# Exponentials of two score blocks per image moved to GpSimd and VectorE, and two kinds of turns moved off TensorE, in a ViT layer with a mixture of experts

## The reference

```
h = patches @ W.T + b + pos_embed                       # 16 images x 1024 tokens x 64
x = layernorm(h)
q, k, v = x @ Wq + bq, x @ Wk + bk, x @ Wv + bv         # 8 heads of 8
scores = q . k / sqrt(8) + col_bias[head, key]          # col_bias from 16384 edges
h = h + softmax(scores) @ v @ Wo + bo
t = layernorm(h)
probs = softmax(t @ router_w.T)                         # 8 experts, the best two are kept
out = h + t + sum_e combine[:, e] * (gelu(t @ w1[e] + b1[e]) @ w2[e] + b2[e])
```

## Time and profile before

| what | value |
|---|---|
| median of 3 runs | 1130.87 us (1130.76 to 1132.0) |
| the profiled execution's own time | 1132.75 us |
| its span, first to last instruction | 1130.7 us |
| TensorE busy (matmuls) | 1086.5 us, 96% |
| ScalarE busy | 1026.2 us, 91% |
| VectorE busy | 623.4 us, 55% |
| GpSimd busy | 130.8 us, 12% |
| mean granted TensorE clock | 0.995 |
| attention stage | about 48 to 991 us |
| expert stage | about 991 to 1130.7 us |

### The profile page before, as it was taken

One profiled execution on the slowest core, in us unless ns is written; L12 is line 12 of the kernel. 1 busy time (PEld: TensorE's weight loads), 2 busy tenths in 40 slices (PEclk: granted clock), 3 DMA queues, 4 the chain that ended last, 5 costly groups with the idle time before them and its releaser, 6 DMA issues.

```text
span 1130.7 us, 21748 instructions
## 1 busy us (share of the span) xinstructions
PE 1086.5 (96%) x7803; PEld 318.6 (28%) x7804; DVE 623.4 (55%) x1765; ACT 1026.2 (91%) x1127; POOL 130.8 (12%) x137
## 2 busy tenths in 40 slices
PE   3499999999999999999999999999999999999998
PEld 3122222222222222222222222222222222233333
DVE  8423465646464737374646465554646542476865
ACT  1299999999999999999999999999999999976654
POOL 3304011111111110102010101010101101000000
PEclk9899999999999999999999999999999999999999
DMA  2523131314141414241423232232323136049895
GB/s 55 128 59 67 55 85 46 88 41 109 30 119 31 107 43 105 46 105 46 104 46 95 56 94 56 74 76 66 84 58 76 42 85 152 16 136 241 236 246 164
DMA packets 73794, 100.78 MB, mean 89 GB/s; under 512 B 17276, under 2 KB 30076, under 8 KB 73660
## 3 DMA queue, kind: packets, MB, share of 16 engines
q1 hardware_dynamic: 71404, 98.73, 34.6%
q10 hardware_dynamic: 1776, 0.24, 0.1%
q0 software_dynamic: 480, 0.06, 0.1%
HBM read 57.67 MB, written 40.37 MB: 87 GB/s over the span
## 4 chain that ended last, share of the span: by engine, by line
PE 77%; ACT 10%; issue 6%; DVE 3%; DMA 2%; SPq 0%; ACTq 0%; POOL 0%; DVEq 0%; POOLq 0%
PE psum L1653 37%; PE psum L1637 21%; ACT probs L1369 10%; PE psum L1706 4%; PE psum L1730 4%; PE psum L743 2%; DMA m_cT<-cT_d 2%; PE psum L731 1%; PE psum L747 1%; PE psum L767 1%; PE psum L772 1%; PE psum L737 1%; PE psum L753 1%; PE psum L1716 1%; DMA x_d<-x2T 0%
## 5 line engine op out<-in xcount | busy, mean ns | idle before, releaser
L1369 ACT ACTIVATE probs<-psum 128x1024 f32<-128x1024 f32 x1024 | 941.1, 1241 | 26.5 <-PE psum L1637 26.4
L1653 PE MATMUL psum<-probs,VA 128*32 128x512 f32 x4096 | 547.0, 606 | 1.9 <-ACT probs L1369 0.4
L1637 PE MATMUL psum<-QA,KA 54*128 54x512 bf16 x2048 | 331.6, 385 | 8.4 <-issue 3.6
L1637 PEld LDWEIGHTS psum<-QA,KA 54*128 54x128 bf16 x2048 | 82.0, 93 | 484.9 <-ACT probs L1369 447.1
L1441 DVE STREAM_TRANSPOSE oT<-psum 128x512 f32<-128x512 f32 x64 | 45.9, 717 | 202.3 <-PE psum L1653 201.8
L1653 PEld LDWEIGHTS psum<-probs,VA 128*32 128x32 f32 x4096 | 81.8, 108 | 151.9 <-issue 130.9
L1404 ACT ACTIVATE probs<-psum,b 128x1024 f32<-128x1024 f32 x64 | 68.1, 1111 | 41.0 <-PE psum L1706 40.9
L1706 PE MATMUL psum<-m_x,w 64*128 64x512 f32 x256 | 61.6, 596 | 2.9 <-DMA m_cT<-cT_d 2.7
L1548 DVE TENSOR_TENSOR probs<-probs,psum 128x1024 f32<-128x1024 f32 x32 | 39.1, 1220 | 33.8 <-PE psum L1716 31.1
L1730 PE MATMUL psum<-probs,w 128*64 128x512 f32 x240 | 57.3, 598 | 0.0
L1308 POOL TENSOR_TENSOR p_rstd<-p_ve,neg_half 128x8 f32<-128x8 f32 x16 | 32.9, 2055 | 207.2 <-DVE p_ve L468 207.2
(11 more groups left out here) (180 smaller groups left out, 813.6 us busy)
## 6 DMA issues: line engine op xcount, KB each, us to landing
H_all<-comb_d SPq DMA_DIRECT2D x64, 256.0 KB, 5.5
QA<-q_parts_d SPq DMA_DIRECT2D x64, 192.0 KB
KA<-k_parts_d SPq DMA_DIRECT2D x64, 192.0 KB
q_parts_d<-qk_parts SPq DMA_DIRECT2D x32, 192.0 KB, 2.5
k_parts_d<-qk_parts SPq DMA_DIRECT2D x32, 192.0 KB, 2.7
xT<-in_xT SPq DMA_DIRECT2D x16, 256.0 KB, 2.7
q_parts_d<-qk_parts SPq DMA_DIRECT2D x32, 128.0 KB, 2.6
k_parts_d<-qk_parts SPq DMA_DIRECT2D x32, 128.0 KB, 2.5
```

The costliest lines, as they stand in the source:

```text
L1369: nc.scalar.activation(probs[:, k % PROB_BUFS, :], score_buf(buf_of(k)), ACT.Exp).then_inc(exped, 1)
L1637: last = pe.matmul(score_buf(buf_of(k))[:, (g % 2) * BANK:(g % 2 + 1) * BANK], KA[rows_of(h, SCORE_ROWS), h // 2, jt * P:(jt + 1) * P], QA ...
L1653: last = pe.matmul(o_acc[32 * g:32 * g + 32, :], VA[:, jt, h, :], probs[:, k % PROB_BUFS, (g % 2) * BANK:(g % 2 + 1) * BANK], start=(jt == ...
```

## The change

Quads 15 and 31 of each image (the last of each half of the heads) give their second block to a side path: `SIDE_QUADS = (15, 31)`, so ScalarE has 62 blocks per image. Its scores are computed by four auxiliary steps of one matmul each (`side_0` to `side_3`), long before the quad's own slot. VectorE drains each to SBUF times log2(e); GpSimd and VectorE then compute 2 to that power on 128x1024 float32: the rounded integer part, the fraction, a polynomial of degree five by ten GpSimd instructions per block in all (six with one tensor input, four with two), and the product with the power of two. The value matmuls of quads 15 and 31 read the result and wait for it (`side_done`).

`norm_t` and `post_t` go: VectorE makes the normalised rows in another order and turns them in 32x32 blocks (`turn_normal`, `turn_x2`), SyncE stores the result to DRAM with four DMAs and loads it as the transposed tile (`store_normal`, `load_normal`, `store_x2`, `load_x2`). `xnT` gets two buffers. The router's matmuls have the weights as the stationary side and write 32 rows each, and VectorE turns the logits. The rows of `comb_d` are stored by one DMA, in another order, in which the loads of L1242 read runs of 128 numbers rather than 512. Slots are moved, and `buf_of` is now a plain remainder counted over all images.

```diff
-BLOCKS = 2 * QUADS
+SIDE_QUADS = (15, 31)
+EXPS = [(q, half) for q in range(QUADS) for half in range(2) if not (half and q in SIDE_QUADS)]
+EXP_OF = {place: k for k, place in enumerate(EXPS)}
+BLOCKS = len(EXPS)
-AUX_SLOTS = {0: ("qk0", 0), 2: ("qk0", 1), 4: ("out_proj", 0), 6: ("out_proj", 1), 8: ("qk1", 0), 10: ("qk1", 1),
-             12: ("post_t", 0), 14: ("router", 0), 16: ("router", 1), 18: ("sq", 0), 19: ("embed", 0), 22: ("embed", 1),
-             24: ("v", 0), 26: ("v", 1), 28: ("combine_t", 0), 30: ("norm_t", 0)}
+AUX_SLOTS = {0: ("side_0", 0), 1: ("side_1", 0), 2: ("qk0", 0), 4: ("qk0", 1), 5: ("out_proj", 0), 7: ("out_proj",
+             1), 10: ("qk1", 0), 11: ("qk1", 1), 13: ("sq", 0), 16: ("side_2", 0), 18: ("side_3", 0),
+             19: ("router", 0), 21: ("embed", 0), 23: ("embed", 1), 25: ("v", 0), 26: ("v", 1), 30:
+             ("combine_t", 0)}
+FRACTION_SLOTS, POWER_SLOTS = (3, 19), (14, 30)
-CENTRE_SLOT, SCALE_SLOT, SPLIT_SLOT, SHIFT_SLOT, LEAD_SLOT, NORM_SLOT = 6, 10, 13, 20, 23, 28
-ROUTER_EXP_BLOCK = 36
-BUF_TURN = 38
+CENTRE_SLOT, SCALE_SLOT, SPLIT_SLOT, SHIFT_SLOT, LEAD_SLOT, NORM_SLOT = 8, 11, 16, 22, 24, 28
+ROUTER_EXP_BLOCK = 38
-COMBINE_SLOT, WEIGH_SLOT = 19, 22
+COMBINE_SLOT, WEIGH_SLOT = 21, 28
-G_SLOT = 26
+G_SLOT = 14
...
+            def side_round(b, side):
+                n = SIDES * b + side
+                g.wait_ge(aux_drained, aux_count(b, SIDE[2 * side + 1]))
...
+                g.tensor_scalar(side_n[:, :], side_y[:, n % 2, :], ROUNDER, None, ALU.add).then_inc(side_rounded, 1)
+            def side_terms(b, side, first, last):
...
+                    if c == 4:
+                        g.wait_ge(side_split, n + 1)
+                        g.tensor_scalar(side_p[:, :], side_f[:, :], POWER_TERMS[5], POWER_TERMS[4], ALU.mult,
+                                        ALU.add).then_inc(side_chain, 1)
+                    else:
+                        g.tensor_scalar(side_p[:, :], side_p[:, :], POWER_TERMS[c], None, ALU.add).then_inc(side_chain, 1)
+                    g.wait_ge(side_chain, base + 2 * (4 - c) + 1)
+                    g.tensor_tensor(side_p[:, :], side_p[:, :], side_f[:, :], ALU.mult).then_inc(side_chain, 1)
+                    g.wait_ge(side_chain, base + 2 * (4 - c) + 2)
+            def side_power(b, side):
+                g.tensor_scalar(side_y[:, n % 2, :].bitcast(I32), side_n[:, :], 1.5 * 2.0 ** 23, 2.0 ** 23, ALU.subtract,
+                                ALU.mult).then_inc(side_ready, 1)
...
+            def side_step(step, b, filled):
+                v.tensor_scalar(side_y[:, n % 2, i % 2 * BANK:(i % 2 + 1) * BANK], aux, LOG2E, LOWEST_POWER, ALU.mult,
+                                ALU.max).then_inc(aux_drained, 1)
+            def side_fraction(b, side):
+                v.wait_ge(side_rounded, n + 1)
+                v.scalar_tensor_tensor(side_f[:, :], side_n[:, :], ROUNDER, side_y[:, n % 2, :], ALU.subtract,
+                                       ALU.subtract).then_inc(side_split, 1)
+            def side_product(b, side):
+                v.wait_ge(side_ready, n + 1)
+                v.scalar_tensor_tensor(side_n[:, :], side_p[:, :], POWER_TERMS[0], side_y[:, n % 2, :], ALU.add,
+                                       ALU.mult).then_inc(side_done, 1)
...
                 link(v.tensor_copy(qk_parts[:, 0, :], qk[:, :]))
-                if bp:
-                    link(v.tensor_tensor(qk_rest[:, :], qk[:, :], qk_parts[:, 0, :], ALU.subtract))
                 v.tensor_tensor(squares[:, :], qk_parts[:, 0, :], qk_parts[:, 0, :],
                                 ALU.mult).then_inc(squares_ready, 1)
+                link(v.tensor_tensor(qk_rest[:, :], qk[:, :], qk_parts[:, 0, :], ALU.subtract))
...
-                    sp.dma_start(comb_d[bq].rearrange("t (r c i) -> c r t i", c=NCH // 2, i=32)[c],
-                                 combB[32 * c:32 * c + 32, :, :]).then_inc(comb_stored, 16)
+                sp.dma_start(comb_d[bq].rearrange("t (p i) -> p t i", i=32), combB[:, :, :]).then_inc(comb_stored, 16)
...
-                        sp.dma_start(wgt_rows[i][D * e:D * e + D, :].rearrange("p (t n) -> p t n", t=2),
-                                     comb_d[b].rearrange("t (e n) -> e t n", e=NX)[2 * m + e].partition_broadcast(D)).then_inc(rows_spread[i], 16)
+                        sp.dma_start(wgt_rows[i][D * e:D * e + D, :].rearrange("p (g n) -> p g n", n=P),
+                                     comb_d[b].rearrange("t (a e n) -> e (t a) n", a=QUARTERS, e=NX)[2 * m + e].partition_broadcast(D)).then_inc(rows_spread[i], 16)
```

The new order on GpSimd, one image:

```diff
                 def body(b):
+                    side_round(b, 0)
+                    if b:
+                        g.wait_ge(pv_done, QUADS * b)
+                        alone(g)
+                        copy_v(1)
                     add_bo(b)
+                    side_terms(b, 0, 4, 3)
                     if b:
                         post_pow(b - 1)
+                    side_terms(b, 0, 2, 1)
+                    side_power(b, 0)
...
                         prep_rq(b + 1)
+                    side_round(b, 1)
+                    side_terms(b, 1, 4, 3)
                     if b + 2 < NB:
                         prep_rstd(b + 2)
+                    side_terms(b, 1, 2, 1)
+                    side_power(b, 1)
```

More of the change, by code:

```diff
@@ L67 @@
 COMB_COPIES = ((0, 24), (24, 48), (48, 64))
-POST_UNITS = {2: "out_proj", 12: "post_t", 16: "router", 32: "combine_t"}
+POST_UNITS = {2: "out_proj", 16: "router", 32: "combine_t"}
 STATS_UNITS = {4: range(NCH // 2), 5: range(NCH // 2, NCH)}
@@ L241, in score_buf, with exp_at, exps_through, values_before @@
             return psum[:, 2 * BANK * i:2 * BANK * (i + 1)]
[L243 to L249, removed]
+        def exp_at(b, q, half):
+            return BLOCKS * b + EXP_OF[q, half]
+        def exps_through(b, q):
+            return exp_at(b, q, 0 if q in SIDE_QUADS else 1) + 1
+        def values_before(n):
+            return QUADS * (n // BLOCKS) + EXPS[n % BLOCKS][0] + 1
         o_acc = psum[:, 6 * BANK:7 * BANK]
@@ L415, in load_shift @@
                                  shift_row[heads, :]).then_inc(aug_loaded[hg], 16)
-            return (load_x, all_parts, first_parts, store_x2, store_tokens, store_combine, store_weights, load_rows, load_zeros,
-                    load_shift)
+            return (load_x, all_parts, first_parts, store_x2, load_x2, store_tokens, store_normal, load_normal, store_combine,
+                    store_weights, load_rows, load_zeros, load_shift)
         def pool_steps(g):
@@ L740, in aux_step @@
                     rows = slice(D * int(step[-1]), D * int(step[-1]) + D)
+                    if step == "qk0" and n >= 2:
+                        pe.wait_ge(xn_loaded, 16 * (n - 1))
                     for i in halves:
                         cols = slice(i * BANK // 2, (i + 1) * BANK // 2)
-                        last = pe.matmul(aux[:, cols], w_qk[rows, :, :].rearrange("k a e -> k (a e)"), xnT[rows, cols],
+                        last = pe.matmul(aux[:, cols], w_qk[rows, :, :].rearrange("k a e -> k (a e)"), xnT[rows, n % 2, cols],
                                          start=True, stop=True)
@@ L746, in aux_step @@
                     for c in chunks:
-                        last = pe.matmul(aux[:, c * P:(c + 1) * P], xnT[:, c * P:(c + 1) * P],
+                        last = pe.matmul(aux[:, c * P:(c + 1) * P], xnT[:, n % 2, c * P:(c + 1) * P],
                                          w_v[:, :, :].rearrange("k t e -> k (t e)"), start=True, stop=True)
-                elif step == "post_t":
-                    pe.wait_ge(x2_made, n + 1)
-                    alone(pe)
-                    for c in range(NCH // 2):
-                        last = pe.transpose(aux[:, c * P:(c + 1) * P],
-                                            x2[:, c, :, :].rearrange("p t d -> p (t d)"), ident[:, :])
                 elif step == "sq":
@@ L1191, in _ @@
                 steps = sync_steps(sp)
-                load_x, all_parts, first_parts, store_x2, store_tokens, store_combine, store_weights = steps[:7]
-                load_rows, load_zeros, load_shift = steps[7:]
+                load_x, all_parts, first_parts, store_x2, load_x2, store_tokens, store_normal, load_normal = steps[:8]
+                store_combine, store_weights, load_rows, load_zeros, load_shift = steps[8:]
                 def body(b):
-                    order = aux_order(b)
+                    if b:
+                        store_x2(b - 1)
+                        load_x2(b - 1)
                     if b + 1 < NB:
@@ L1277, in _ @@
                         load_weights(u + 2 * WEIGHT_BUFS - 2)
-                    if POST_UNITS.get(u - 1) == "post_t":
-                        sp.wait_ge(aux_drained, END + POST.index("post_t") + 1)
+                    if u == SCALE_UNIT + 1:
                         store_x2(NB - 1)
+                        load_x2(NB - 1)
```

(2 more changed lines are left out.)

283 lines of the change are left out of this document (191 added, 92 removed).

## The result

The changed kernel takes **1392.94 us** (median of 4 runs, 1391.74 to 1400.45), the kernel before 1131.43 us beside it: a ratio of 1.232, with a 95% interval of 1.229 to 1.235. It is 23% slower; forecast were 1112 us, with a range up to 1180.

A forecast was written before the change was run, and what follows sets the result against it. It took ScalarE (58.3 us) and TensorE (57.6 us), coupled by three score buffers, to bound the 58.8 us image. 1132.75 - 25.6 + 5 + 1.6 = 1113.8, with the median 1.9 lower: 1112 us, range 1100 to 1180.

The forecast's parts named there:

- The shared path: GpSimd and VectorE meeting in SBUF: perhaps ten meetings of 0 to 2.4 us, taken as 0.3 us per image, 5 in all.
- the two-input price: GpSimd operation with two inputs: 2.39 us for 1024 elements, upper end for the one-input float operations taken at 1.1.
- The second rival: GpSimd and VectorE take turns, TensorE waits for VectorE: 0 to 9 us per image, 1177 to 1250 us; chance 0.33.
- 0.908 us in a chain: ScalarE in attention: 62 exponentials per image, one following the other, 56.4 us of work, 1.8 less.
- the sum of -1.2 us: TensorE per image: transposes and router halves removed, new router, single scores and evacuation wait added, leaving 56.4 us of work.
- about 7: VectorE per image: drains, three-operand steps and turns, less two copies, add about 7 us, making 39.5 of 57.2.
- The period: Time per image in attention: 56.4 us on both engines plus 0.8 gives 57.2, 1.6 less, 25.6 for 16 images.
- SyncE at cost 0: SyncE's DMA queue: the added stores and loads of normalised rows and x2 delay nothing that is due, cost 0.
- Experts, +1.6: Expert stage: TensorE loses 1.4 us of work, weight rows read in shorter runs cost +3, net +1.6 us.
- the third rival: Expert stage: weight rows arrive late, DMA at its limit, +12 to +35 us, 1125 to 1147; chance 0.10.

The follow-up runs named there:

- experiment 6: k1 with one side block per image and the low part's split in slot 18, chain on VectorE (k5) or GpSimd (k6): 1147.1 and 1217.1 us.
- experiment 3: The kernel before with ten GpSimd products per image that nobody reads, or twice as many fills instead: 1255.3 and 1131.7 us.
- Experiment 1: The changed kernel with GpSimd's additions written as product and addition, and the last step likewise: 1348.3 us.
- k1: The kernel without a side block from experiment 4, with the load of normalised rows moved ahead in SyncE's queue: 1148.1 us, ratio 1.012.
- experiment 2: The changed kernel without the side path, 64 exponentials back on ScalarE, router, turns and slots kept: 1160.5 us.
- experiment 4: The changed kernel with weights stored in eight DMAs; no side block, one on GpSimd (fast forms), or one on VectorE: 1234.2, 1312.4, 1261.6 us.
- k5: k1 with one side block per image, whole chain on VectorE, split of the low part in slot 18: 1147.1 us, ratio 1.013.
- k6: k1 with the same side block and split slot as k5, but the chain on GpSimd in fast forms: 1217.1 us, ratio 1.075.

## Why the prediction was wrong

**The step that failed is "The shared path".** It had the right mechanism, from the right rows, and counted ten meetings of up to 2.4 us an image; then it put them down as 0.3 us, because "most fall where nothing is due". The side path as a whole cost 75.0 - 59.8 = 15.2 us per image against the kernel without one: TensorE waits for 12.5 us where it waited for 1.9, and is busy for 62.5 where it was for 57.9. What the runs put in its place is three things.
- Meetings don't fall here and there. GpSimd's chain is back to back, and so is VectorE's between a drain and a due point, so step after step of VectorE meets the next of GpSimd: scale, cast and squares in a row add 2.2 + 1.7 + 0.7 us (experiment 6). The argument that VectorE is idle for 26 us of an image was of no use: experiment 3 lost 9 us per image with VectorE far from full. A short step is lengthened like a long one: `comb`, 0.23 us before, takes 2.08 ahead of the wait for `combine_t`.
- The size of one meeting was too small as well. The bound of 2.4 us held for the products only; operations of 2.8 to 3.6 us were priced at 1.1, from the range's lower end. The text had given the two-input price as its upper end, and that too was passed. Experiment 1 puts this at 45 us of the total: in the fast forms GpSimd is busy for 39.7 us per image, where 39 were forecast, in the changed kernel for 59.
- A wait of TensorE was priced at its own length. A long one costs more, since the granted clock falls behind it (below).

**The second rival** (0.33) had the mechanism and the places, `sq` and the ranking with `combine_t` behind it; its upper price, 9 us per image, was too low for 15.2. The last two of these points and the wait for the side block itself (2.15 us), which it did not name, are what it lacks. The sign that the prediction set for it, gaps over 1 us on TensorE and 0.69 us steps stretched to over 2, is what the profile shows.

**ScalarE** does have 62 exponentials, but not at 0.908 us in a chain: it waits 268.8 us for scores. **TensorE**: the sum of -1.2 us cannot be read from the changed kernel. Without the side path TensorE is busy for 580.84 / 600 x 59.8 = 57.9 us against 58.7, 0.8 less, where the parts without the side block's own additions had promised 2.0. **VectorE**: the terms of its sum make 8.1 us, not "about 7"; nothing hangs on it. **The period**: with the removed transposes and 64 exponentials it is 59.2 in k1, not below 58.8, so moving the router and the turns off TensorE bought nothing; exponentials come 0.2 to 0.6 us late at blocks 11, 38 and 53. That steps in neighbouring slots are the cause wasn't shown: the kernel with spaced steps had other waits.

**SyncE at cost 0**: right for the changed kernel, with no room. TensorE waits for `xnT` there for no time worth listing, for up to 1.2 us once the side path is gone, and 4.2 us once seven stores more stand ahead of the load.

**Experts, +1.6**: in fact 158.9 - 140.8 = 18. Weight loads land in 6.7 us for 5.5, under the 7 that the third rival set as its sign, and TensorE waits 10.7 us for `m_cT` where it waited 2.7. The excess of 16.5 over the term lies inside that rival's price (12 to 35), but its mechanism, the weight rows, has the smaller part. From the last exponential to the end it is 155.4 us with short runs and no side path (experiment 2) and 150.2 with long ones (experiment 4, landing in 5.4): the runs are worth about 5 us. The other kernels with long runs have 149.2 to 152.5, and k1 has 156.1, in an execution that was 7 us above k1's median. With long runs TensorE still waits 8 to 13 us for `m_cT`. In experiment 4's kernel without a side block these are two waits, 4.05 and 4.90 us, and SyncE's queue stands ahead of each. Before the first, it issues the stores of `store_x2` for the last image (1104.56), waits 2.8 us for them to land, issues `load_x2` (1109.24), and the load of `m_cT` comes at 1113.57; the kernel before has no such turn. Before the second stand the eight stores of weights, 5.4 us where the four of before took 1.86. No run changed this order in the expert stage, so that the queue is the cause there is argued from these rows, not shown.

## What to carry over

Before work that reads SBUF is handed to GpSimd, list VectorE's steps with two SBUF inputs and its fast casts that stand between an arrival and a due point, and count with up to a whole GpSimd instruction more for each; VectorE's idle share says nothing about it. If the work must move, VectorE itself can be the cheaper place, with each piece put behind the step that TensorE waits for. The same holds for an in-order DMA queue: every issue ahead of an urgent load is 0.4 to 0.7 us of its wait.

## What the hardware showed

**A long wait of TensorE is paid about twice.** Windows of the kernel after, before and behind the 2.44 us wait that ends at 717.94:

```profile
710.00:714.00 4.00, 4.00 (x32) 0.82 (x36) 3.83 (x9) 3.63 (x5) 3.92 (x2) 1.00 0.18 37
718.00:722.00 4.00, 4.00 (x22) 0.77 (x22) 0.56 (x2) 1.02 (x1) 3.91 (x2) 0.50 0.24 61
722.00:726.00 4.00, 3.82 (x21) 0.59 (x17) 1.96 (x2) 2.29 (x3) 2.24 (x2) 0.70 0.71 185
726.00:734.00 8.00, 7.83 (x57) 2.41 (x57) 4.99 (x8) 7.58 (x9) 6.14 (x4) 1.00 0.48 100
```

The granted clock is 0.50, the lower of its two levels (1.2 GHz), for four microseconds and more, and 22 matmuls start in 4 us where 32 did. Behind k5's wait of 1.66 us it stays at 1.00; behind k6's of 4.31 it is 0.50 for 4 us and 0.76 for the next 4. So of the 64.3 - 59.3 = 5.0 us per image between k5 and k6 only 2.65 are wait, and TensorE's longer busy time is the rest: 553.75 / 600 x 64.3 = 59.3 us against 575.38 / 600 x 59.3 = 56.9. In the changed kernel it is 62.5 against 57.9 in experiment 2's. The Trainium skill, TensorE: Matmul & The Clock Gate, "Part 1: The HAM clock gate", says that the gate has these two levels only; the 0.50 and 1.00 agree, and 0.70 is a mean over a change.

**The form of a GpSimd operation matters more than its arithmetic.** With 128x1024 float32, multiply by 1 and add takes 1.05 to 1.12 us, an addition alone 2.78 to 2.91; with an int32 result, multiply and add 1.20 to 1.37 against 3.64 for subtract and multiply. Which property of the slow forms does it wasn't tried.
